# Cross attention on one core: the order of ScalarE's copies around the high part of P

## The reference

```
x_q = w_qk y, transposed          x_k = w_qk x          x_v = w_v x + b_v
energy    = x_q x_k               (1024 x 1024)
attention = softmax of each row; then each column divided by (1e-07 + its sum)
x_r       = x_v attention         (256 x 1024)
out       = x + relu(w_t (x - x_r) + b_t)
```

## Time and profile before

| | |
|---|---|
| runs before, us | 1952.18, 1953.07, 1953.61; median 1953.07 |
| profiled execution, its own time | 1952.44 us |
| its span, first to last instruction | 1950.6 us, 26266 instructions |
| mean granted TensorE clock | 0.995 of full speed |
| busy share of the span | PE 97%, PEld 80%, DVE 77%, ACT 67%, POOL 42% |
| chain that ended last, by engine | PE 93%, issue 3%, ACT 2%, DVE 1% |

### The profile page before, as it was taken

The page is one execution under the profiler, slowest core; times in us unless marked ns, Lnnn a source line. Parts: engine busy times, 40 slices in busy tenths (PEclk is TensorE's granted clock), DMA queues, the critical chain, the costliest instruction groups (busy, mean ns, idle before and its releaser), DMA issues.

```text
span 1950.6 us, 26266 instructions
## 1 busy us (share of the span) xinstructions
PE 1894.3 (97%) x8928; PEld 1558.6 (80%) x8928; DVE 1502.3 (77%) x1836; ACT 1307.8 (67%) x1793; POOL 812.7 (42%) x424
## 2 busy tenths in 40 slices
PE   6999999999999999999999999999999999999998
PEld 5878888878888788887788887888878888878886
DVE  5787777877777877778777787777787777877776
ACT  4677666776666766667766667666677666676664
POOL 6534444433445344444344453444433444433430
PEclk8999999999999999999999999999999999999999
DMA  2011111111111111101111111111011111111100
GB/s 103 23 65 44 66 65 34 52 43 65 65 52 34 59 49 65 65 25 61 43 65 65 43 43 48 59 65 65 22 65 43 65 65 43 43 43 65 65 22 22
DMA packets 33657, 101.91 MB, mean 52 GB/s; under 512 B 4176, under 2 KB 4944, under 8 KB 33616
## 3 DMA queue, kind: packets, MB, share of 16 engines
q1 hardware_dynamic: 33072, 101.46, 14.9%
q10 hardware_dynamic: 544, 0.00, 0.0%
HBM read 67.90 MB, written 33.55 MB: 52 GB/s over the span
## 4 chain that ended last, share of the span: by engine, by line
PE 93%; issue 3%; ACT 2%; DVE 1%; DMA 0%; ACTq 0%; SPq 0%; DVEq 0%
PE pv L624 36%; PE row_b L539 18%; PE row_a L539 11%; PE pv L602 9%; PE row_b L594 5%; PE row_a L594 5%; PE row_b L585 5%; PE row_a L585 5%; ACT ev L284 1%; DVE res L470 0%; ACT p_hi L301 0%; DMA x_sb<-x 0%; DVE row_inv L419 0%; PE row_a L631 0%; DVE hnT_lo L515 0%
## 5 line engine op out<-in xcount | busy, mean ns | idle before, releaser
L194 POOL TENSOR_TENSOR y_lo<-y_raw,y_hi 128x896 fp32r<-128x896 f32 x128 | 307.0, 2399 | 978.5 <-ACT y_hi L256 978.5
L293 ACT ACTIVATE p_sb<-p_sb,neg_max 128x1024 f32<-128x1024 f32 x256 | 294.4, 1153 | 70.0 <-DVE neg_max L411 70.0
L429 DVE SCALAR_TENSOR_TENSOR colsum<-p_sb,row_inv,colsum 128x1024 f32<-128x1024 f32 x224 | 334.8, 1495 | 8.2 <-DVE row_inv L419 0.4
L284 ACT ACTIVATE ev<-row_b 128x512 f32<-128x512 f32 x384 | 228.1, 594 | 163.5 <-PE row_b L539 163.5
L301 ACT ACTIVATE p_hi<-p_sb,row_inv 128x1024 fp32r<-128x1024 f32 x256 | 293.2, 1146 | 62.6 <-PE pv L624 57.0
L436 DVE SCALAR_TENSOR_TENSOR p_lo<-p_sb,row_inv,p_hi 128x1024 fp32r<-128x1024 f32 x256 | 316.9, 1279 | 0.0
L411 DVE CUSTOM_DVE_ANT_0 p_sb<-row_a,ev 128x1024 f32<-128x1024 f32 x128 | 156.8, 1225 | 207.0 <-PE row_a L539 207.0
L624 PE MATMUL pv<-p_hi,z_hi 128*128 128x512 f32 x1024 | 275.8, 391 | 0.0
L624 PE MATMUL pv<-p_hi,z_lo 128*128 128x512 f32 x1024 | 274.2, 389 | 0.0
L624 PE MATMUL pv<-p_lo,z_hi 128*128 128x512 f32 x1024 | 273.7, 389 | 0.0
L539 PE MATMUL row_b<-gx_hi,y_hi 128*128 128x512 f32 x512 | 210.4, 411 | 37.4 <-ACT ev L284 35.4
(11 more groups left out here) (99 smaller groups left out, 3643.2 us busy)
## 6 DMA issues: line engine op xcount, KB each, us to landing
x_sb<-x SPq DMA_DIRECT2D x64, 512.0 KB, 4.0
out<-res SPq DMA_DIRECT2D x64, 512.0 KB, 2.9
y_raw<-y SPq DMA_DIRECT2D x64, 256.0 KB, 3.7
y_raw<-y SPq DMA_DIRECT2D x32, 512.0 KB, 3.8
res<-w_qk SPq DMA_DIRECT2D x1, 256.0 KB, 3.8
res<-w_t_T SPq DMA_DIRECT2D x1, 256.0 KB, 7.0
res<-w_v SPq DMA_DIRECT2D x1, 256.0 KB, 7.0
bv_sb<-b_v ACTq DMA_DIRECT2D x1, 1.0 KB, 4.0
```

What stands on the lines that cost most here:

```text
L194: nc.gpsimd.tensor_tensor(y_lo[:, :, cols], y_raw[:, 1:8, cols], y_hi[:, :, cols].bitcast(FP32), ALU.subtract).then_inc(y_lo_done, 1)
L284: nc.scalar.activation(ev[:, to, :], bank_b, ACT.Copy, scale=scale).then_inc(b_copied, 1)
L293: nc.scalar.activation(p_sb[r][:, :], p_sb[r][:, :], ACT.Exp, scale=-1.0, bias=neg_max[:, j:j + 1], accum_out=row_sum[:, j:j + 1]).then_in ...
L429: nc.vector.scalar_tensor_tensor(out=colsum[:, :], in0=p_sb[r][:, :], scalar=inv, in1=colsum[:, :], op0=ALU.mult, op1=ALU.add).then_inc(ac ...
```

## The change

Only the order of ACT's instructions changes; all the instructions, their operands, their waits and all other engines stay as they are. `p_high` of a pair's second tile (r=1) is taken from the end of its own slot in slots 1 to 3 and issued inside the next slot. In slot 2 it comes after `copy_b` n=0, `copy_e` and `copy_b` n=1; in slots 3 and 4 it comes after `copy_b` n=0 and ahead of `copy_e` and `copy_b` n=1. In slot 4 the pair's own second `p_high` stays at the end of the slot, since no slot of the batch follows.

```diff
                 if t == 0:
                     copy_b(b, t, 1, EV_U2, -1.0)
                     act.wait_ge(t_lo_done, 2 * b + 2)
-                copy_e(b, t)
-                if t > 0:
+                    copy_e(b, t)
+                elif t == 1:
+                    copy_e(b, t)
+                    copy_b(b, t, 1, EV_U2, -1.0)
+                    p_high(b, t - 1, 1, first)
+                else:
+                    p_high(b, t - 1, 1, first)
+                    copy_e(b, t)
                     copy_b(b, t, 1, EV_U2, -1.0)
                 if t > 0 and not last:
                     y_high(b + 1, t - 1)
...
                 exponent(b, t, 0)
                 exponent(b, t, 1)
                 p_high(b, t, 0, first)
-                p_high(b, t, 1, first)
+                if t == NP - 1:
+                    p_high(b, t, 1, first)
```

## The result

The changed kernel takes 1908.18 us (median of 4 runs, 1907.15 to 1909.99) against 1952.62 before (1951.54 to 1953.61, the three runs of the table and one more): ratio 0.9775, 95% interval 0.9763 to 0.9787, a gain of 44.4 us. The profiled execution took 1907.15, with a span of 1905.4. The forecast was 1910, a gain of 43.2.

A forecast was written before the change was run, and what follows sets the result against it. PE, 97% busy, was taken to bound the kernel. 31 x 1.32 + 1.04 + 64 x 0.02 = 43.2 us off the profiled 1952.44 gave 1909.2; the median, 0.6 above, 1909.9, given as 1910; range 1906 to 1918.

The forecast's parts named there:

- The hole in slot 2: PE's gap before `p6`, waiting for ACT's `copy_b` n=0: it closes whole, gaining 1.32 us in each of 31 batches.
- Nothing is late next in slot 2: Slot 2's later work costs nothing: `energy_out` comes 0.56 us late against PE, covered by slack of 0.73.
- The slack forecast for slot 3's first copy: In slot 3, 0.73 us of slack before the first copy is due at T + 0.88 covers the delay from slot 2.
- Slots 3 and 4: copy n=1 at T + 2.92, cost nothing, no cover left: ACT's `copy_b` n=1, counted from the slot's first matmul T, arrives just when `p6` is done, at no cost.
- Rival A: `p7` turns late in slots 3 and 4: 6.4 us per 0.1 us of longer ACT chain, 1913 to 1919; chance 0.12.
- The small gain, 64 x 0.02: At `p6` in slots 3 and 4, an earlier copy removes 0.02 us between the first two matmuls, 64 times: 1.3 us.
- The further 0.03 at `p7`: Perhaps another 0.03 us gained at `p7`, 96 times, 3 us; not in the sum, only in the range's lower end.
- The sum: All gains over the whole run: 31 x 1.32 + 1.04 for the first batch + 64 x 0.02 = 43.2 us.
- Rival B: No change: slot 2's late `p_low` meets POOL's `y_low`, DVE suffers and the gain is given back, 1953; chance 0.02.
- Rival C: Slower: in slots 3 and 4 `copy_e` and `copy_b` n=1 queue behind a `p_high` awaiting the row inverse, 1971; chance 0.03.

The follow-up runs named there:

- e1: The changed kernel with the new order in slot 2 only, slots 3 and 4 taken back to the order before: 1909.75 us, ratio 0.9779.
- e3: The changed kernel with the moved `p_high` between `copy_b` n=0 and `copy_e` in slot 2 too: 1919.92 us, ratio 0.983.
- e4: The changed kernel with the moved `p_high` behind `copy_b` n=1 in slots 3 and 4 too: 1967.2 us, ratio 1.0074.
- e7: The changed kernel with `p3` before `p7` on PE and `x_high` ahead of copy n=2 on ACT in slots 3 and 4: 1921.84 us, ratio 0.9843.
- e6: The changed kernel with PE doing `p3` before `p7` in slots 2 to 4: 1928.43 us, ratio 0.9877.
- e8: e6 with POOL also waiting, before the batch's last `y_low`, until DVE has done the last `p_low`: 1900.25 us, ratio 0.9732.
- e10: The changed kernel with POOL also waiting, before the batch's last `y_low`, until DVE has done the last `p_low`: 1908.04 us, ratio 0.9775.

## Why the prediction was right

- *The hole in slot 2 closes whole, 1.32 us.* Right: 1.33, from the stretches, and `e1` shows that this alone brings 1909.75. The working took it from both sides (the copy's advance, and PE's own pace at 942.30 against 942.31); the trace shows that the two meet (`p6` 0.23 behind `p2`, and 0.17 behind the end of the copy, 921.50).
- *Nothing is late next in slot 2.* Right. The slack forecast for slot 3's first copy, 0.73, is 0.69 in the trace.
- *Slots 3 and 4: copy n=1 at T + 2.92, cost nothing, no cover left.* Right to the hundredth, with some luck: the three distances were taken as 0.50, 1.06 and 0.48 and are 0.49, 1.04 and 0.51, so that their errors cancel. That there is no cover is shown by `e3`, where 0.37 of delay cost 0.37 each time. Rival A did not come about because the distances of the earlier trace rows hold for the new neighbours to within 0.03, and their sum exactly. The estimate from the page ScalarE: Activation LUTs (Trainium skill, section What ACT_TABLE_LOAD costs) was 2.08 for the three distances; the trace has 2.04, and the measurement decides: the 2.6 us that the page would have cost did not appear.
- *The small gain, 64 x 0.02.* The one term that was mis-sized: slots 3 and 4 give 2.0 us together. The 0.02 at `p6` went as forecast (931.98 to 932.20, 0.23), but in slot 3 the matmuls behind it had been slower too. From `p6` to `p7` slot 3 took 1.65 us before (953.93 to 955.58) and takes 1.58 now:

```profile
931.98 0.39 PE L546 MATMUL row_b<-gx_hi,y_hi 128*128 128x512 f32 x1
932.20 0.39 PE L546 MATMUL row_b<-gx_lo,y_hi 128*128 128x512 f32 x1
...
933.56 0.45 PE L546 MATMUL row_b<-gx_hi,y_hi 128*128 128x512 f32 x1
933.85 0.39 PE L546 MATMUL row_b<-gx_lo,y_hi 128*128 128x512 f32 x1
```

- *The further 0.03 at `p7`*, held possible in each of 96 slots, went the other way: the distance between `p7`'s first two matmuls was 0.25 in slots 2 and 3 and 0.28 in slot 4, and is now 0.28 to 0.29 in all three. The lower end of the range stands a little low besides: 1909.9 less 3 is 1907, not 1906.
- *The sum.* The slots give 42.65 + 1.22 + 0.82 = 44.7 us against a forecast of 43.2; the medians of the runs differ by 44.4, the span by 45.2.
- *Rival B* was rightly called covered here, but the reason was incomplete. "Nothing in the rows is that long" was a statement on this order alone. In slot 2 `y_low` does meet the moved `p_low`, but starts 0.88 behind it, and it is `y_low` that lengthens (2.14 to 2.39 us, POOL in the stretches). `e4` shows `p_low` pairs of 4.35 us, one small move away, and PE stands for it at the end of the batch, not at the next `p1`.
- *Rival C* did not occur: no idle time of ACT for the row inverse before the moved `p_high` in the changed kernel. The only wait of `p_high` left is the 18.7 us in 32 of the last one in a batch, which was not moved.

## What to carry to other kernels

Where an engine with an in-order queue feeds the bounding engine, first look at what stands ahead of the feeding instruction without being needed so soon; the gain is the distance by which it moves forward, and it can be read to a few hundredths from starts (not durations) of neighbours. Then ask how far the displaced instruction may go: here two copies later, in two slots of four, cost 59 us through two other engines whose instructions lengthen each other. A reorder that is right by itself can lose by such a meeting, and a wait that keeps the two apart tells it in one run.

## What the hardware showed that was not expected

- Between DVE's `p_low` (two large SBUF operands) and POOL's `y_low`, 0.1 us decides who pays. Where the second `p_low` starts 0.10 ahead of POOL, it keeps its 1.28 us and `y_low` is stretched from 2.13 to 3.17. Where `y_low` starts within 0.01 of it (`e7`) or 0.27 to 0.33 ahead (`e6`, `e4`), `y_low` takes 2.12 to 2.40 and the two `p_low` 4.34 to 4.39 instead of 2.48; the pair then ends 1.1 us after `y_low` does (`e4`, `e6`, `e7`), so most of the second `p_low` ran behind it. The changed kernel is 0.10 us away from that, and so was the kernel before. DVE and POOL in the kernel before:

```profile
973.58 2.48 DVE L436 SCALAR_TENSOR_TENSOR p_lo<-p_sb,row_inv,p_hi 128x1024 fp32r<-128x1024 f32 x2
```

```profile
974.87 3.19 POOL L194 TENSOR_TENSOR y_lo<-y_raw,y_hi 128x896 fp32r<-128x896 f32 x1 [3.67 <-ACT y_hi L256]
```

The Trainium skill, SBUF — State Buffer, section Who interferes with whom, says that the order of issue and not the form of the operation decides who is blocked; this case's traces agree: 3.15 us for the second `p_low` behind `y_low` (`e4`), 3.17 us for `y_low` behind it (the changed kernel).
- A copy that comes late for `p7` costs more than the gap that the timeline shows. With `p7` in time, the nine matmuls of `p7`, `p3` and `p4` take 9 x 0.227 = 2.04; in the changed kernel they take 2.13 (923.27 to 925.40), 0.09 more, of which only 0.05 are at the first. In `e8` nearly all of it came back: 7.8 us less than `e10` on the same chip, 0.08 for each of 96 slots. Why the later ones are slower is open.
